# A transformer step on one core: the input in four row blocks, one block for norm, queries and q', and the first softmax among the q' products

## What is computed

```python
q = (x @ Wq).reshape(b, n, HEADS, DIM_HEAD)
k = (context @ Wk).reshape(b, m, HEADS, DIM_HEAD)
v = (context @ Wv).reshape(b, m, HEADS, DIM_HEAD)
sim = jnp.einsum('bihd,bjhd->bhij', q, k) * SCALE
attn = jax.nn.softmax(sim, axis=-1)
out = jnp.einsum('bhij,bjhd->bihd', attn, v).reshape(b, n, HEADS * DIM_HEAD)
return out @ Wout + bout
```

## Time and profile before

| | us |
|---|---|
| median of three runs | 1759.29 (1759.19 to 1769.43) |
| span of the profiled execution, the only time that the profile gives for it | 1761.3 |
| TensorE busy | 1654.4 (94% of the span) |
| DVE, ACT, GpSimd busy | 1001.3, 584.0, 357.7 |
| first real matmul of the queries | 15.02 |
| first matmul of unit 0's scores, of unit 1's | 44.33, 56.79 |
| first matmul of unit 0's weighing | 67.36 |

### The profile page before, as it was taken

How to read it: one execution, slowest core, us unless ns; L and a number is a source line. 1 busy time by engine, 2 the same in 40 slices (tenths; PEclk the granted TensorE clock), 3 DMA queues, 4 the chain that set the end, 5 groups by cost and what they waited for, 6 DMA issues and landing times. The chain is left out here.

```text
span 1761.3 us, 23423 instructions
## 1 busy us (share of the span) xinstructions
PE 1654.4 (94%) x8900; PEld 1288.9 (73%) x8900; DVE 1001.3 (57%) x1541; ACT 584.0 (33%) x1064; POOL 357.7 (20%) x327
## 2 busy tenths in 40 slices
PE   7999999999998989997999998989899999999996
PEld 3899999999995777874556565758686666666672
DVE  4569678777684634456999997574526530000014
ACT  3353454444531211012544442144346521111110
POOL 1431432233031020011454543300200010000010
PEclk9899999999999979998898988999999999999998
DMA  5232132223113568557254452150101197696860
GB/s 171 77 101 68 57 112 67 94 65 113 57 43 127 197 222 286 182 178 272 91 180 170 156 199 104 39 202 1 44 8 49 39 340 275 219 330 217 320 208 31
DMA packets 113044, 251.45 MB, mean 143 GB/s; under 512 B 14726, under 2 KB 44438, under 8 KB 108182
## 3 DMA queue, kind: packets, MB, share of 16 engines
q1 hardware_dynamic: 104352, 230.72, 37.9%
q10 hardware_dynamic: 6006, 10.62, 1.7%
q0 software_dynamic: 2560, 8.39, 1.4%
HBM read 230.95 MB, written 18.75 MB: 142 GB/s over the span
## 5 line engine op out<-in xcount | busy, mean ns | idle before, releaser
L457 PE MATMUL x_s_ps<-x_cxt,x_qs 128*128 128x400 f32 (+1 forms) x1152 | 244.5, 357 | 7.6 <-ACT x_pr L599 4.1
L1246 PEld LDWEIGHTS e_ps<-e_xg,e_w 128*128 128x128 f32 x1792 | 206.7, 192 | 33.3 <-issue 33.1
L486 PE MATMUL x_o_ps<-x_cx,x_pt 128*128 128x386 f32 (+1 forms) x1248 | 228.0, 340 | 1.0 <-DVE x_o L588 1.0
L486 PEld LDWEIGHTS x_o_ps<-x_cx,x_pt 128*128 128x128 f32 (+1 forms) x1248 | 218.1, 188 | 2.6 <-DVE x_o L588 1.2
L1246 PE MATMUL e_ps<-e_xg,e_w 128*128 128x128 f32 x1792 | 209.4, 276 | 7.2 <-issue 6.3
L457 PEld LDWEIGHTS x_s_ps<-x_cxt,x_qs 128*128 128x128 f32 x1152 | 205.8, 192 | 8.8 <-issue 4.4
L1238 PE MATMUL e_ps<-e_w,xt 128*128 128x512 f32 x352 | 160.4, 597 | 1.4 <-DMA e_w<-in_L_ffn_W 1.4
L2440 PE MATMUL x_s_ps<-x_cxt,x_qs 128*128 128x512 f32 (+1 forms) x384 | 141.3, 525 | 2.8 <-ACT x_sc L2561 1.7
L1485 DVE TENSOR_TENSOR e_y<-e_ps,e_b 128x512 f32<-128x512 f32 x20 | 13.7, 687 | 204.7 <-PE e_ps L1238 204.7
L2440 PEld LDWEIGHTS x_s_ps<-x_cxt,x_qs 128*128 128x128 f32 x384 | 67.9, 194 | 79.8 <-issue 79.0
L535 DVE TENSOR_TENSOR x_pt<-x_t_ps,x_pt 128x512 fp32r<-128x512 f32 x124 | 72.5, 587 | 90.8 <-ACT x_pt L619 90.3
(11 more groups left out here) (444 smaller groups left out, 2719.0 us busy)
## 6 DMA issues: line engine op xcount, KB each, us to landing
e_w<-in_L_ffn_W SPq DMA_DIRECT2D x16, 4096.0 KB, 16.0
x_cxt<-in_ctxT SPq DMA_DIRECT2D x8, 2401.5 KB, 9.2
x_cx<-in_ctx SPq DMA_DIRECT2D x8, 2304.0 KB
e_w<-in_L_ffn_gate_up_proj SPq DMA_DIRECT2D x8, 2048.0 KB, 8.4
x_stage<-in_ctxT SPq DMA_DIRECT2D x16, 768.0 KB, 4.5
x_stage<-in_ctx SPq DMA_DIRECT2D x16, 768.0 KB, 6.0
e_w<-in_L_ffn_down_proj SPq DMA_DIRECT2D x8, 1024.0 KB, 9.5
x<-in_ctxT SPq DMA_DIRECT2D x8, 768.0 KB, 4.3
```

Of the source, the lines that this page charges most:

```text
L457: last = nc.tensor.matmul(s_ps[:, n, 0:b - a], qs[:, u % 2, p, c, :], cxt[:, q, c, a:b], start=(m + c == 0), stop=(m + c == len(PARTS) + C ...
L486: last = nc.tensor.matmul(o_ps[:, 0:WIDE], pt[0:rows, p, t, :], cx[0:rows, q, t, :], start=(t + m == 0), stop=(t + m == KT - 1 + len(PARTS ...
L1246: last = nc.tensor.matmul(u_ps[:, g % 2, a * PER + n, :], w1[:, e % PAIR, m, a * hidden + c * P:a * hidden + (c + 1) * P], xg[:, m, :], st ...
```

## The change

- x is loaded in four transfers, one per row block, each with its semaphore, and the waits for x as a whole and for the identity in a block of their own are gone. Loads of weights and of the first two key pieces follow at once in the same block. Since x is still in use then, these two pieces go to the two slots of `stage`; pieces 2 and 3 go to the slots in x, and SP issues them only when all four blocks are normed.
- Blocks 1 to 4 become one. The norm goes row block by row block (`BlockNorm`), with DVE's statistics of the next block between.
- ACT casts all four key pieces, DVE makes all four low parts in this block (two were in block 5, and GpSimd cast two).
- After 12 of the 24 q' products TensorE makes unit 0's 36 matmuls of scores, then the other 12. Row maximum and exponent of unit 0 stand among DVE's and ACT's copies of these; GpSimd makes the operands of units 0 and 1 in this block.
- The wait for the fills of `cx` goes from the scores of unit 0 to its weighing.
- The PSUM banks of both blocks are one tile `ps` in the change, so `x_s_ps`, `x_t_ps` and `n_tps` of before are all `x_ps` there.
- Some semaphores of the expert stages are made only where they are used.

```diff
-        slots = (lent[:, 0:PIECE], stage[:, 0, :], stage[:, 1, :], lent[:, PIECE:TT * D])
+        slots = (stage[:, 0, :], stage[:, 1, :], lent[:, 0:PIECE], lent[:, PIECE:TT * D])
...
+        pr = core.sb(both, "x0_pr", [P, CTX])
+        nmost = core.sb(both, "x0_nmost", [P, 2])
+        nmax = core.sb(both, "x0_nmax", [P, 2])
+        ps = core.pb(both, "x0_ps", [P, 8, 512])
+        s_ps, t_ps, o_ps, ot_ps = ps[:, 0:GR, :], ps[:, GR:GR + 2, :], ps[:, 6, :], ps[:, 7, :]
...
+            norm = BlockNorm(core, c2, "n0", x, xn)
...
+            EARLY = 2 * 2 * CC
...
+                    rows = w["x"].rearrange("(t p) n -> p t n", p=P)
+                    for t in range(TT):
+                        sp.dma_start(x[:, t, :], rows[:, t, :]).then_inc(rows_in[t], 16)
+                    sp.dma_start(ident[:, :], w["ident"]).then_inc(ident_in, 16)
                     sp.dma_start(wq[:, :, :], w["L0_xattn_Wq"].rearrange("(c p) n -> p c n", p=P)).then_inc(wq_in, 16)
-                    sp.dma_start(wkt[:, :, :], w["L0_xattn_WkT"].rearrange("(c p) n -> p c n", p=P)).then_inc(wq_in, 16)
-
-            normalise()
-            ps = core.pb(c2, "x0_ps", [P, 8, 512])
-            with nc.Block() as block:
-                @block.sync
-                def _(sp):
-                    for n in range(GR):
-                        load(sp, 0, n)
+                    load(sp, 0, 0)
+                    sp.dma_start(wkt[:, :, :], w["L0_xattn_WkT"].rearrange("(c p) n -> p c n", p=P)).then_inc(wk_in, 16)
+                    load(sp, 0, 1)
+                    sp.wait_ge(norm.normed_ready, TT)
+                    load(sp, 0, 2)
+                    load(sp, 0, 3)
                     filters.load(sp)
...
+                    pe.wait_ge(ident_in, 16)
+                    for n in range(IDLE):
+                        nc.tensor.transpose(tps[:, TT - 1, n % KC, :], ident[:, :], ident[:, :])
+                    for t in range(TT):
+                        pe.wait_ge(norm.normed_ready, t + 1)
+                        for c in range(KC):
+                            last = nc.tensor.transpose(tps[:, t, c, :], xn[:, t, c * P:(c + 1) * P], ident[:, :])
+                        last.then_inc(turn_ready, 1)
+                    pe.wait_ge(wq_in, 16)
+                    pe.wait_ge(xt_ready, TT)
...
+                    pe.wait_ge(wk_in, 16)
                     for n in range(H * CC):
+                        if n == EARLY:
+                            pe.wait_ge(pad_ready, 1)
+                            pe.wait_ge(qt_ready, KC)
+                            for g in range(GR):
+                                scores(pe, 0, g)
...
+                    for t in range(TT):
+                        act.wait_ge(turn_ready, t + 1)
+                        nc.scalar.copy(xt[:, :, t * P:(t + 1) * P], tps[:, t, :, :]).then_inc(xt_ready, 1)
+                    high_part(act, 0, 0)
+                    high_part(act, 0, 1)
                     for m in range(KC):
                         act.wait_ge(q_ready, m + 1)
                         nc.scalar.mul(qt[:, m, :], ps[:, m, :], DH ** -0.5).then_inc(qt_ready, 1)
-                        if m in (1, 2):
-                            high_part(act, 0, m - 1)
+                        if m < 2:
+                            high_part(act, 0, m + 2)
                     for n in range(H * CC // 2):
+                        if n == EARLY // 2 + 2:
+                            exponent(act, 0)
...
+                    for t in range(TT):
+                        dve.wait_ge(rows_in[t], 16)
+                        norm.feed(dve, t)
+                        if t:
+                            norm.scaled(dve, t - 1)
+                    norm.scaled(dve, TT - 1)
+                    for n in range(GR):
+                        low_key(dve, 0, n)
                     for n in range(H * CC // 2):
+                        if n == EARLY // 2:
+                            row_max(dve, 0)
...
+                    norm.begin(pool)
+                    for t in range(TT):
+                        norm.deviation(pool, t)
+                    pool.wait_ge(ident_in, 16)
...
-                    pool.wait_ge(lowt_ready, 2)
-                    for n in range(2, GR):
-                        slot, high, _ = piece(n)
-                        pool.wait_ge(piece_in[n], 16)
-                        nc.gpsimd.tensor_copy(high, slot).then_inc(high_ready, 1)
-                    pool.wait_ge(even_used, CC)
-                    pool.wait_ge(odd_used, CC)
-                    queries(pool, 0)
+                    for u in range(2):
+                        pool.wait_ge(even_used, (u + 1) * CC)
+                        pool.wait_ge(odd_used, (u + 1) * CC)
+                        queries(pool, u)
...
-                    queries(pool, 1)
...
-                    pe.wait_ge(pad_ready, 4)
...
+                        else:
+                            pe.wait_ge(pad_ready, 4)
...
-                    low_key(dve, 0, 2)
-                    low_key(dve, 0, 3)
...
-                    exponent(0)
...
+            ctx, f"{name}s", "s_ready b_ready g_ready half_ready shifted x_done x_out") if shared else [None] * 7
+        added, smooth, turned = core.sems(ctx, f"{name}m", "added smooth turned") if not gated else [None] * 3
...
-        x_in, = core.sems(ctx, "io", "x_in")
         sent = nc.dram_tensor("sent", (TILES * P, D), F32, kind="Internal").ap()
         back = nc.dram_tensor("back", (TILES * P + P, D), F32, kind="Internal").ap()
-        with nc.Block() as block:
-            @block.sync
-            def _(sp):
-                sp.dma_start(x[:, :, :], w["x"].rearrange("(t p) n -> p t n", p=P)).then_inc(x_in, 16)
-                sp.dma_start(ident[:, :], w["ident"]).then_inc(x_in, 16)
-                sp.wait_ge(x_in, 32)
```

91 lines of the change are left out of this document (39 added, 52 removed).

## The result

| | before | changed |
|---|---|---|
| median of 10 runs, us | 1763.91 (1759.19 to 1769.43) | 1757.22 (1746.32 to 1777.34) |
| ratio, 95% interval | | 0.9941 (0.9914 to 0.9969) |
| span of the profiled execution, granted clock | 1761.3 | 1758.3, 0.967 |

The change makes the kernel 0.59% faster (0.31 to 0.86%); on 1763.91 us that is 10.4 us (5.5 to 15.2). The interval leaves out 1, and the gain is smaller than the 1% that the forecast used as its bound for "no change". The spread of single runs of the changed kernel, 31 us, is three times the gain. The median of before was 1759.29 on three runs and is 1763.91 on ten; the forecast of 1749.5 stood on the first.

What follows compares the result with a forecast made beforehand. TensorE was taken to run without pause from 74 us on, so gains ahead of unit 0's weighing (67.36 us) carry to the end; -2.4 - 7.6 - 0.2 + 0.4 = -9.8, a median of 1749.5 us, range 1744 to 1757.

Steps and rivals of the forecast that it cites:

- Start, -2.4: Load and norm of x by row blocks: queries start at 12.6 us instead of 15.02, a gain of 2.4 us.
- rival of late quarters: Start: row blocks land together or late, or block-wise norm eats the gain; queries stay at 15.0, median 1751.9; chance 0.10.
- Queries, q', scores, no term: Queries 13.9 us, first 12 q' products 5.95, unit 0's scores 6.84 at full clock; keys and operand in time.
- fifth rival: A key piece or the operand comes after 32.5 us and the products wait; no gain, 1759 us; chance 0.04.
- Second half of the q' products, -7.6: Softmax of unit 0 under the second 12 products removes both pauses; queries to unit 1's scores 34.2 us, gain 7.6.
- The value piece, -0.2: Unit 1's scores to unit 0's weighing: third value piece, issued behind the barrier, causes a 2.5 us pause; net gain 0.2.
- third rival: The value piece isn't waited for and the start comes at 11.4 us; gain 13.5, median 1745.8; chance 0.10.
- Clock, +0.4: Half-loaded second half of the q' products and the 2.5 us pause: some slow clock, a loss of 0.4 us.
- second rival: Clock falls in the sparse stretch or the 2.5 us pause, unit 1's scores run slow; median 1753.3; chance 0.14.
- Sum to the weighing: All terms ahead of unit 0's weighing together: it should start near 57.5 us instead of 67.36.
- Fourth rival, slow stretches behind: The shift makes two more slow-clock stretches of 8.6 us each in the expert stage; 1766.7 us; chance 0.04.
- All later stages of the length they have now: Sign in the changed profile: stages behind 68 us keep their lengths; wrong if they differ by more than 3 us.

Runs made afterwards that it cites:

- e_one_load: The changed kernel with x loaded in one piece, all else still by row blocks; ratio to the kernel before 0.9937.
- e_value_early: The changed kernel with all four value pieces of unit 0 asked for in the first block; median 1760.93 us, ratio to the kernel before 0.9949.
- e_no_idle: The changed kernel without the fourteen idle transposes on the identity ahead of the real ones; ratio to the kernel before 0.9925.
- e_ident_first: The changed kernel with the identity loaded ahead of the rows of x instead of behind them; ratio to the kernel before 0.9967.
- e_again: The changed kernel once more, no edit; median 1762.18 us, ratio to the kernel before 0.9940.
- e_start_only: The changed kernel with unit 0's scores, maximum and exponent back at the head of the block of units, behind all fills; ratio to the kernel before 0.9998.
- e_best: The changed kernel without the fourteen idle transposes and with all four value pieces of unit 0 asked for in the first block; median 1749.86 us, ratio 0.9920.
- e_both: The changed kernel with the identity loaded ahead of x and all four value pieces of unit 0 asked for in the first block; ratio 0.9960.

## Why the prediction was right, step by step

- **Start, -2.4.** Measured 12.80 against 12.6. The reason holds: the fourth block's transposes follow the idle ones (9.69) and the norm (10.0) at once. What was missing is that this point scatters: 12.05, 12.80 and 14.20 in three executions of the same kernel, the last beyond the 14 that I had named as a sign of being wrong. It scatters with the landing of the identity and the speed of the transposes behind it. The rival of late quarters (15.0) falls; quarters, issued some 0.45 apart, have the first statistics at 3.50, against 5.8 at which the whole of x lay in SBUF before (0.72 and 5.1). In e_one_load, with one transfer, they start at 6.23. The Trainium skill's rule of at least 1 MiB per DMA ("DMA: Bandwidth & Descriptors", Rules for kernel authors) did not decide here. The 2 us of fixed cost that I took from its anatomy of one DMA are given there for transfers issued by GpSimd; these were issued by SP.
- **Queries, q', scores, no term.** 13.97, 5.96 and 6.83 against 13.9, 5.95 and 6.84. The keys and the operand were in time: no pause ahead of 32.59. That is the fifth rival's end.
- **Second half of the q' products, -7.6.** Right mechanism, 0.5 too good: 34.70 from the queries to the next block instead of 34.2, so -7.1. The second twelve products with their last copy took 7.7 behind the scores instead of 7.2, and the barrier 0.5 instead of 0.3.
- **The value piece, -0.2.** Right: a pause of 2.14 where 2.5 was forecast, for the reason given, and gone in e_value_early. That is the third rival's end.
- **Clock, +0.4.** Nothing: PEclk is 1.00 at 45 us and in the pause, and the scores behind it take 1.88 to 1.90 for nine. The second rival did not come here; but in e_no_idle (3.24 for nine), in e_ident_first (2.69) and in e_one_load (2.75) it did in part, at the same place. The length of the pause ahead doesn't decide it: 2.14 us in the changed kernel and 1.76 in its repeats left the clock up, 1.83, 1.93 and 1.91 in those three did not. So that the term came out at nothing is in part luck, and the rival was closer than the 0.14 I gave it suggests. The Trainium skill, "TensorE: Matmul & The Clock Gate", The HAM clock gate, has activity as what releases the clock; the 13.97 and 16.86 us for the same queries agree with that.
- **Sum to the weighing.** Forecast 57.5, measured 57.84 (56.7 and 58.9 in the repeats).
- **Fourth rival, slow stretches behind.** In the changed kernel's own execution the last expert stage has 28.3 us at the lower clock instead of 13.8 and is 8.3 us longer, near the 8.6 that this rival counts for one slow stretch; in the repeats it has 13.9 and 21.0. It comes and goes without an edit, so nothing points to a cost of the shift.
- **What the sum left out.** Between the weighing and the end of the first cross attention 0.9 us is lost in the changed kernel, as in every run with its unit loop. Two units before, and two after:

before:

```profile
310.12 7.12 PE L486 MATMUL x_o_ps<-x_cx,x_pt 128*128 128x386 f32 x39
325.31 7.12 PE L486 MATMUL x_o_ps<-x_cx,x_pt 128*128 128x386 f32 x39
340.50 1.82 PE L486 MATMUL x_o_ps<-x_cx,x_pt 128*128 128x386 f32 x9
```

after:

```profile
301.05 7.13 PE L536 MATMUL x_ps<-x_cx,x_pt 128*128 128x386 f32 x39
316.25 7.14 PE L536 MATMUL x_ps<-x_cx,x_pt 128*128 128x386 f32 x39
331.50 0.78 PE L536 MATMUL x_ps<-x_cx,x_pt 128*128 128x386 f32 x3
```

Units follow each other at 15.19 and 15.19 before, and at 15.20 and 15.25 after, with no wait in the trace, and so from the second unit to the last. A few hundredths in every second unit, 31 units, make the 0.9. Its cause is open: the change made one PSUM tile of three and moved several buffers, and neither was undone alone. "All later stages of the length they have now" was wrong in this small thing, and for the experts and the cross attention of layer 1 wrong by more than the 3 us that I had named, through scatter that e_again shows to be there without any edit.
- **The total.** The forecast gain was 9.8 us and the measured one is 10.4 (5.5 to 15.2). That they lie 0.6 apart is partly luck: the traces show 8.7 us at the end of the first cross attention (7.7 and 9.8 in the repeats), and the interval would have held anything from 5.5 to 15.2. The level was 4.6 us off: three runs of before gave 1759.29, ten gave 1763.91, and 1763.91 - 9.8 is 1754.1. So 1757.22 stands 0.2 us beyond the end of my range, although the difference came as forecast. I also took 2.0 us off the span for what lies around it; the changed kernel's profiled execution took 1760.13 on a span of 1758.3, that is 1.8 more, not less. The range should have carried the uncertainty of a median of three runs that spread over 10 us.

## What to carry to other kernels

A pause of TensorE can cost twice, once as time and once as slow work behind it (here after 3.54 and 4.09 us it did, after 2.14 it did not); putting the row maximum and exponent of a unit under matmuls that are ready takes both away (here 7.5 us out of 67 alone). When a pause goes, read which transfer is issued behind a barrier: here it was the next pause, and issuing it one block earlier took that away in the trace (2.26 us, of which 0.7 came back a unit later). And where single runs spread by 30 us, judge an edit of 2 us by the stage that it touches, in the trace, with a repeat of the same kernel beside it, since neither the total nor one profile can.

## What the runs showed of the hardware that was not expected

**A small operation on GpSimd waits beside DVE.** The same fill of 128x13, before (beside a subtraction on DVE that starts at the same 41.84 and takes 1.76) and after (with DVE idle):

```profile
41.84 1.84 POOL L418 TENSOR_SCALAR x_cx<-ident 128x13 fp32r<-128x13 f32 x1 [7.32 <-POOLq L327]
41.84 1.76 DVE L293 TENSOR_TENSOR x_cxt<-x_stage,x_cxt 128x1536 fp32r<-128x1536 f32 x1 [0.32 <-PEq L327]
```

```profile
47.35 0.22 POOL L484 TENSOR_SCALAR x_cx<-ident 128x13 fp32r<-128x13 f32 x1 [12.24 <-POOLq L361]
```

It takes 1.84 us instead of 0.22. The same fill takes 0.22 in e_start_only too (at 39.12), where it stands ahead of the scores as before but beside no subtraction. These 1.6 us are nearly half of the first pause of the earlier trace rows and nearly all by which it shrinks, from 3.54 to 1.83, in e_start_only without any edit of the fill. This was read from traces and not isolated. The Trainium skill, "SBUF — State Buffer", Who interferes with whom, calls the pair of ports that DVE and GpSimd share an exclusive lock, and has a DVE instruction with two inputs in SBUF contend with a GpSimd one that reads SBUF. The subtraction has two such inputs, the fill reads `ident`, and it ends when the subtraction does (43.68 and 43.60): the trace agrees. I had not weighed it in the prediction, where the fill's 1.84 stood in the pause as if it were its own length.

**The clock column can miss the slow start.** In e_best, and in e_both likewise, the column reads 1.00 from 11.8 to 15.8, but the weight loads of the queries come 0.85 us apart there and 0.43 apart later:

```profile
12.99 0.34 PEld L394 LDWEIGHTS x_ps<-xt,x_wq 128*128 128x128 f32 x1 [0.52 <-issue]
13.84 0.34 PEld L394 LDWEIGHTS x_ps<-xt,x_wq 128*128 128x128 f32 x1 [0.52 <-issue]
...
17.00 0.19 PEld L394 LDWEIGHTS x_ps<-xt,x_wq 128*128 128x128 f32 x1 [0.26 <-issue]
17.43 0.19 PEld L394 LDWEIGHTS x_ps<-xt,x_wq 128*128 128x128 f32 x1 [0.24 <-issue]
```

```profile
11.80:15.80 4.00, 3.80 (x5) 1.77 (x6) 1.76 (x1) 1.53 (x2) 0.00 (x0) 1.00 1.05 385
```

In e_ident_first, with the same pitch, it reads 0.50. So at the start of these kernels the column missed the lower clock in two traces of three, and the pitch of equal instructions told it in all.
